# A state-space layer beside two layers of local attention: softmax division moved to GpSimd, and orders of their own for the first and last chunks

## What is computed

```
branch 1 (512 inner channels, 16 states):
  xz = x_n @ in_proj.T ; x_in, z = split(xz)
  xc = silu(conv4(x_in) + b) ; B, C, dt_low = split(xc @ x_proj.T)
  dt = softplus(dt_low @ dt_proj.T + bias)
  h[t] = exp(dt[t] * A) * h[t-1] + dt[t] * xc[t] * B[t]
  y[t] = sum_states(h[t] * C[t]) + D * xc[t]
  out1 = (y * silu(z)) @ out_proj.T
branch 2, for each of 2 layers (8 heads of 64, windows of 128 tokens):
  q, k, v = shift(x) @ wqkv ; q, k = rotate(l2norm(q)), rotate(l2norm(k))
  p = softmax(q k^T + mask) over the own and the previous window
  x = x + (p v) @ wo
  x = x + (a * gelu(g)) @ w2, with a, g = layernorm(shift(x)) @ w1
```

## Time and profile before

| | |
|---|---|
| median of 3 runs | 2378.99 us |
| lowest and highest | 2377.95 and 2399.59 us |
| profiled execution | 2396.66 us, span 2394.9 us |
| instructions | 37640 |
| granted TensorE clock, mean | 0.957 |
| DMA | 388.52 MB, mean 162 GB/s |

### The profile page before, as it was taken

How to read it: one execution, slowest core, us unless ns; L and a number is a source line. 1 busy time by engine, 2 the same in 40 slices (tenths; PEclk the granted TensorE clock), 3 DMA queues, 4 the chain that set the end, 5 groups by cost and what they waited for, 6 DMA issues and landing times. The chain is left out here.

```text
span 2394.9 us, 37640 instructions
## 1 busy us (share of the span) xinstructions
PE 2111.3 (88%) x10944; PEld 1346.1 (56%) x10944; DVE 2070.7 (86%) x2948; ACT 1602.0 (67%) x3895; POOL 895.7 (37%) x1038
## 2 busy tenths in 40 slices
PE   6589898998899989899888998889889898998788
PEld 2355565655556556565555645655556655656456
DVE  2889898998889988899888989889888998899983
ACT  3666676767666766668667676776766666777662
POOL 1343333343433433244333343334342433333430
PEclk9799999999999999999999999999999999999899
DMA  3467675677666766667756776657765677666762
GB/s 120 119 160 200 161 186 139 155 191 188 145 171 146 188 186 147 157 166 174 188 133 169 185 166 176 142 159 197 170 152 135 166 198 165 183 163 150 186 151 56
DMA packets 113130, 388.52 MB, mean 162 GB/s; under 512 B 11408, under 2 KB 32272, under 8 KB 94368
## 3 DMA queue, kind: packets, MB, share of 16 engines
q0 software_dynamic: 46080, 151.02, 35.6%
q1 hardware_dynamic: 66848, 235.10, 29.6%
HBM read 238.75 MB, written 155.71 MB: 165 GB/s over the span
## 5 line engine op out<-in xcount | busy, mean ns | idle before, releaser
L614 DVE TENSOR_TENSOR_SCAN hb<-dA,state,hb 128x512 f32<-128x512 f32 x512 | 672.9, 1314 | 14.8 <-ACT dA L843 3.1
L1044 POOL DMA_DIRECT2D ysum<-dA x256 | 223.9, 892 | 556.6 <-DVE dA L621 507.0
L1028 POOL COPY state<-hb 128x2 f32<-128x2 f32 x256 | 209.7, 819 | 560.5 <-DVE hb L614 560.4
L843 ACT ACTIVATE dA<-dt_sb,amat 128x512 f32<-128x512 f32 x512 | 349.0, 721 | 98.4 <-DMA ysum<-dA 97.0
L949 ACT ACTIVATE probs<-ring,nmax 128x256 f32<-128x256 f32 x512 | 235.9, 478 | 227.0 <-DVE nmax L719 226.8
L1308 PE MATMUL ring<-hT,w 128*128 128x256 f32 (+1 forms) x1536 | 347.9, 382 | 6.6 <-ACT hT L970 6.5
L1308 PEld LDWEIGHTS ring<-hT,w 128*128 128x128 f32 (+1 forms) x1536 | 268.2, 178 | 83.3 <-issue 24.4
L924 ACT ACTIVATE rot<-rot,rnorm 128x64 f32<-128x64 f32 x1024 | 256.4, 339 | 82.7 <-POOL rnorm L1109 80.5
L621 DVE TENSOR_TENSOR dA<-hb,bc 128x1024 f32<-128x1024 f32 x256 | 310.8, 1214 | 0.0
L607 DVE TENSOR_TENSOR hb<-u_sb,bc 128x1024 f32<-128x1024 f32 x256 | 307.4, 1201 | 1.2 <-DMA bc<-bc_rows 1.2
L1109 POOL TENSOR_TENSOR rnorm<-rnorm,powers 128x8 f32<-128x8 f32 x128 | 235.3, 1838 | 23.5 <-POOL rnorm L1106 23.5
(11 more groups left out here) (118 smaller groups left out, 3464.7 us busy)
## 6 DMA issues: line engine op xcount, KB each, us to landing
bc<-bc_rows SPq DMA_DIRECT2D x128, 1024.0 KB, 5.9
ysum<-dA POOLq DMA_DIRECT2D x256, 512.0 KB, 7.0
wqkv<-in_wqkv SPq DMA_DIRECT2D x48, 512.0 KB, 8.3
w<-in_w SPq DMA_DIRECT2D x16, 1364.0 KB, 13.9
w<-in_w SPq DMA_DIRECT2D x16, 768.0 KB, 6.8
tab<-in_tab SPq DMA_DIRECT2D x64, 128.0 KB, 7.3
ysum<-xconv POOLq DMA_DIRECT2D x32, 256.0 KB, 4.2
wo<-in_wo SPq DMA_DIRECT2D x16, 512.0 KB, 11.9
```

The source lines that it names most:

```text
L614: dve.tensor_tensor_scan(hb[:, k % H_RING, :], dA[:, k % DA_RING, :], hb[:, k % H_RING, :], state[:, k:k + 1], ALU.mult, ALU.add).then_inc ...
L843: act.activation(dA[:, k % DA_RING, :], dt_sb[:, j, :], ACT.Exp, scale=amat[:, n:n + 1]).then_inc(dA_ready.sem, 1)
```

## The change

It has two parts.

The division. `spread`, ScalarE's copy to `rb`, and VectorE's product into `oT` are gone, with the tile `rb` and its signal. In their place GpSimd multiplies each head's exponentials by the reciprocal of its row sum, in place, eight instructions of 128x256 for a window (512 in all), before TensorE transposes them; TensorE's transposes wait for that (`probs_scaled`). VectorE's reciprocal now waits for the scalings of the window before in place of the spread. `obank` is copied to `oT` by ScalarE (`attended`, `o` in its order).

The orders. All five steady lists are new, and each engine has a list for the first pass and one for the last: `passes_of` gives the first list once (in it a word without a plus is chunk 0, one plus chunk 1), the steady list for c from 0 to 5, and the last list for c = 6 (plain is chunk 6, one plus chunk 7). `load_y` waits for one semaphore more: that GpSimd has saved the halo of the next chunk.

The core of the diff; of the lists, which are some 200 lines, the parts that the text speaks of:

```diff
+def passes_of(first, steady, last):
+    return [(first, 0), *((steady, c) for c in range(CHUNKS - 2)), (last, CHUNKS - 2)]
...
-    rb_ready = Signal("rb_ready", NA)
+    probs_scaled = Signal("probs_scaled", HEADS * NA)
...
                     sp.wait_ge(*filled(min(it + 1, CHUNKS - 1), ("conv", j)))
                     sp.sem_inc(passed, 1)
+                    sp.wait_ge(*halo_saved.at(min(it + 1, CHUNKS - 1), 1))
+                    sp.sem_inc(passed, 1)
                     sp.wait_ge(*gated.at(it - 1, j + 1))
...
             def invert(a):
                 dve.wait_ge(*probs_ready.at(it, (a + 1) * HEADS))
-                dve.wait_ge(*filled(it if a else it - 1, ("rb", (a - 1) % NA)))
+                dve.wait_ge(*probs_scaled.at(it, a * HEADS))
                 dve.reciprocal(rinv[:, :], rowsum[:, :]).then_inc(rinv_ready.sem, 1)
-            def heads_out(a):
-                dve.wait_ge(*o_done.at(it, (a + 1) * PAIRS))
-                dve.wait_ge(*rb_ready.at(it, a + 1))
-                dve.wait_ge(*filled(it if a else it - 1, ("wo", (a - 1) % NA)))
-                dve.tensor_tensor(oT[:, :, :], obank[:, :].rearrange("p (a t) -> p a t", a=NJ), rb[:, :, :],
-                                  ALU.mult).then_inc(oT_ready.sem, 1)
...
-            def rb_out(a):
-                act.wait_ge(*filled(it, ("rb", a)))
-                act.wait_ge(*oT_ready.at(it, a))
-                act.activation(rb[:, :, :], bank(it, ("rb", a))[:, :].rearrange("p (a t) -> p a t", a=NJ), ACT.Copy)
+            def attended(a):
+                act.wait_ge(*o_done.at(it, (a + 1) * PAIRS))
+                act.wait_ge(*filled(it if a else it - 1, ("wo", (a - 1) % NA)))
+                act.activation(oT[:, :, :], obank[:, :].rearrange("p (a t) -> p a t", a=NJ), ACT.Copy)\
+                   .then_inc(oT_ready.sem, 1)
...
+            def scale_probs(a, g):
+                pool.wait_ge(*rinv_ready.at(it, a + 1))
+                pool.sem_inc(passed, 1)
+                for odd in range(2):
+                    head = 2 * g + odd
+                    pool.tensor_scalar(probs[:, g, odd, :], probs[:, g, odd, :], rinv[:, head:head + 1], None,
+                                       ALU.mult).then_inc(probs_scaled.sem, 1)
...
             def flip_probs(a, g):
-                pe.wait_ge(*probs_ready.at(it, a * HEADS + 2 * g + 2))
+                pe.wait_ge(*probs_scaled.at(it, a * HEADS + 2 * g + 2))
...
-            def spread(a):
-                pe.wait_ge(*rinv_ready.at(it, a + 1))
-                pe.wait_ge(*freed(it, ("rb", a)))
-                for h in range(HEADS): ...
...
-        for c in range(-AHEAD, CHUNKS):
-            run_pass(PE_ORDER, of_chunk, c)
+        for order, c in passes_of(PE_FIRST, PE_ORDER, PE_LAST):
+            run_pass(order, of_chunk, c)
```

379 lines of the change are left out of this document (249 added, 130 removed).

## The result

| | before | after |
|---|---|---|
| median, same chip | 2378.91 us (4 runs) | 2644.43 us (4 runs) |
| lowest and highest | 2377.95 to 2399.59 | 2639.44 to 2646.98 |
| profiled execution | 2396.66, span 2394.9 | 2646.20, span 2644.4 |
| granted TensorE clock, mean | 0.957 | 0.894 |

The ratio of the times is 1.109, with a 95% interval of 1.103 to 1.115. The forecast was 2329 us and its range ended at 2420.

The account below looks back on a forecast made before the run. TensorE (88%) and VectorE (86%) were nearly full together, neither the bound alone; -28 us steady and -22 at the ends made -50 from 2396.66, 2346.7 profiled, 2329 us on the median, range 2265 to 2420.

Parts of the forecast that it names:

- Added on GpSimd: GpSimd: 512 scalings of 128x256 at an estimated 0.52 us, 266 us, taking it from 895.7 to 1162 us busy.
- Waits, costed at zero on average: Transposes behind exponentials, reciprocal and two scalings, state copies behind scalings in GpSimd's queue: zero, since the orders place consumers later.
- GpSimd's queue is late: Rival, chance 0.13: longer scalings make TensorE wait 96 us against 66 saved; 2387 us, from 2355 to 2430.
- What they cost VectorE: VectorE's scans and products held up by GpSimd's scalings: 0.16 us each, 82 us in all, bounds nothing and 225.
- The shared port takes more than the change gives: Rival, chance 0.17: scalings beside VectorE's scans and products cost 0.34 us each, giving 2417, or 2461 at 0.44.
- Removed work, and the DMA waits: Per chunk: 8.3 us off TensorE (spread), 6.7 off VectorE (products), and half of VectorE's 13.3 DMA waits, 6.6.
- the last rival: Rival, chance 0.06: VectorE's DMA waits go wholly and the port costs little; -14.9 us a chunk, 2253 us.
- The forecast's own -4.0: Steady part, us a chunk, chosen near VectorE's -3.1 against TensorE's -8.3; -28 us over seven periods.
- The ends: First pass -10 us (bounds 0 and -25) and last pass -12 (0 and -30), together -22 us.
- SP's new wait for the halo: SP's queue: the load of y waits for the saved halo, expected to be saved long before; zero.
- The later condition: TensorE's transposes wait for all eight exponentials and the reciprocal, where they began after the first pair; costed at zero.
- The cover: GpSimd, 37% busy, stays under half of the span with the scalings, 74% at worst: not the bound by share.

Follow-up runs that it names:

- the memset's 5.7: Kernel after the change, each scaling replaced by a memset of 560 idle columns waiting for the one before (division missing): 2290.30 us, ratio 0.956.
- a window of 1.5 us: Kernel after the change, each scaling replaced by a memset of one column of an idle tile (division missing): 2242.91 us, ratio 0.935.

## Why the prediction was wrong, point by point

**Added on GpSimd: the step that failed first.** The prediction put a scaling at 0.52 us alone, with 0.311 and 0.726 as its bounds. It takes 0.92, outside them. The argument was that an operation with one input is cheaper than one with two. On this engine it isn't (0.92 against 0.61 to 0.72 for 256 columns). At the least duration in place, 0.912, 512 of them are 467 us, and they are 707 busy in place, not 266.

**Waits, costed at zero on average: the step that decided.** The prediction described the chain rightly (exponentials, reciprocal, scalings, transposes; state copies queued behind) and as a rival, "GpSimd's queue is late", gave it 0.13 and up to 2430 us. It set two scalings ahead of the first transposes, 1.0 us by its price, and costed no wait for the other six. But a pair of scalings takes 2.4 us in the timeline and a pair's four transposes 0.66, so TensorE stands between pairs until the eighth is done. A window of 8 x 0.52 = 4.2 us would have been hidden for the most part if it had stayed so short: the memset's 5.7 costs 47 us in all. But it would not have. Eight scalings of eight columns, 0.30 us each with VectorE idle, made a window of 8.2 and cost 170 us, and 128 columns, 0.60 each, cost 286. So a right price of 0.52 would not have saved the forecast: what it lacked is that each scaling is lengthened by 0.54 to 0.60 us on average beside VectorE, and that TensorE waits for all eight. The rival for the late queue had this for the longest operations only and left 1.5 us of wait a window; it is 5.0. Three costs came together: 321 us of TensorE waiting for scaled exponentials; the busy time of the transposes and head products, 129 us over the kernel without scalings, about 100 of it the lower clock after standing (the estimate above); and VectorE's 106 us for state copies behind the scalings. They overlap in part; the whole is 400.

**What they cost VectorE: wrong the other way.** Forecast 82 us, 0.16 for each scaling. Measured against the earlier trace rows: 512 x 0.017 + 256 x 0.050 + 256 x 0.039 = 32 us. "The shared port takes more than the change gives" was the rival with the most chance, and not what happened. When the two meet, GpSimd's operation is the one that becomes much longer (0.92 alone to 1.51 in place; 0.30 to 0.84 with eight columns). All 235 scalings that started while VectorE ran a scan or one of the two products lasted over 1.1 us, those under a scan 2.48 at the median; with VectorE idle the median is 0.918. VectorE's own loss is small: the 137 scans that started under a running scaling have a mean of 1.392 against a median of 1.277 for those that met none. The two-input form costs VectorE more, about 0.19 us each over the kernel without scalings (512 x 0.063 + 256 x 0.141 + 256 x 0.118 = 99 us), near the prediction's 0.16. The prediction had a row of the one side, a table product that held up a scan by 0.44 us, and took that for the common case; the 1.73 us of the longest table product was the sign of the other, and it was used for the late queue alone, as an exception. The Trainium skill (SBUF — State Buffer, section "SBUF: two separate sides") has the two engines exclude each other there, the one that starts first keeping the port and the other blocked for the whole instruction. The runs agree for GpSimd as the second (the eight-column operations above), and differ on what VectorE pays as the second: 32 us over 512 scalings are 0.06 us each, where full blocking had given the rival its 0.34.

**Removed work, and the DMA waits: right in kind, too small.** Without the scalings the distance between two chunks falls from 288.1 to 272.4 us (five steady periods of the same copy), 15.7 a chunk. That is nearly what the last rival had put together, 8.3 in both engines' views and 6.6 more for DMA waits that go wholly, 14.9; its time was 2253, measured 2244 (2220 on the chip of the forecast, by the ratio). The forecast's own -4.0 had halved the DMA waits and taken off the port's cost. After, the same distance is 322.7 us ((2128.0 - 514.6) / 5): 50.3 longer for eight windows, 6.3 each.

**The ends** gave 29 us (forecast 22). **SP's new wait for the halo**, costed at nothing, cost nothing that shows: no wait for y is left on VectorE. **The later condition** for the transposes, costed at nothing, is shown to be free.

**The cover.** GpSimd at 37% looked like room. The share says that the engine can do more in a chunk; it says nothing on whether it can do it within the few microseconds in which TensorE's list has something else. That time is bounded by the runs: a window of 1.5 us is hidden wholly, 5.7 mostly, and of what is above 8 nothing is.

**Open.** Not tried: lists planned anew for scalings of 0.91 us (more of TensorE's work between the reciprocal and the transposes), the old lists with the new division, and how the 400 us divide between the three costs, since no run here removes the clock's part alone.

## What to carry to other kernels

Before work is moved to an idle engine, measure its exact form there, alone and beside what the neighbouring engine will run: bounds from neighbouring forms did not hold, "fewer inputs" was no bound at all, and the price alone was three fifths of the price in place. Then price the serial stretch that a consumer waits for (here 8 operations, 64 times) against the work that the consumer's list has in that time, rather than the total against the engine's idle share. And count what else the waiting costs: the queue behind the moved work, and TensorE's clock after it stood. When a change couples a new mechanism with a new order, run each alone: here the order was a gain of 2.5% with the old mechanism, hidden under a loss.

## What the runs showed of the hardware that was not expected

- GpSimd, f32, 128 partitions, alone: product with one scalar for each partition, 256 columns 0.92 us, 128 columns 0.60; the same as a two-input product with that scalar broadcast 0.61 for 256. The slower form is the one with fewer inputs.
- GpSimd operations that read SBUF become longer beside VectorE's scans and its products with both inputs in SBUF, by a mean of 0.54 to 0.60 us each whatever their length (eight columns: 0.30 to 0.84, eight in 6.79 us). Beside VectorE's rotation products out of PSUM they stay at 0.305. Memsets of 560 columns, which read nothing, stay at 0.565 median; those of one column had a median of 0.098, and of 0.43 when they started under the product before the scans.
- VectorE loses little to one-input scalings (scan 1.309 without them, 1.331 with), more to the two-input form (1.372; its two products 1.222 and 1.214 without, 1.363 and 1.332 with).
- TensorE stood 2.40, 1.15, 1.13 and 0.69 us in front of four groups of transposes; the clock fell to the lower level (1.2 GHz) during the second stand and stayed there for 10.24 us, and four transposes took 1.11 us in place of 0.66. Over the run the mean clock fell from 0.957 to 0.894.
